# Expert tiles: a third weight buffer, and a ring of six chunks for the activations' parts

## The reference, cut to what matters

```
B, P, D, D_MLP, E, K = (2, 256, 128, 512, 8, 2)     # B is 16 in this run
gate_logits = jnp.einsum('bpd,de->bpe', x, W_gate)
top_w, top_idx = jax.lax.top_k(gate_logits, K)
...
for e in range(E):
    h = jax.nn.gelu(jnp.einsum('bpd,dm->bpm', x, W_in[e]) + b_in[e], approximate=False)
    y = jnp.einsum('bpm,md->bpd', h, W_out[e]) + b_out[e]
    out = out + combine[..., e, None] * y
```

## Time and profile before

| | |
|---|---|
| median of the runs | 4289.31 us |
| profiled execution | 4290.81 us |
| its span | 4289.0 us, mean granted clock of TensorE 0.963 |
| first two phases | to 3872 us |
| staging, gate, attention of the experts phase | 3872 to 4046 us |
| tile loop | 4046 to about 4256 us |
| last scatters, sums and the store | to 4289 us |
| PE busy over the span | 3967.9 us (93%) |
| DVE, ACT, POOL busy | 3516.5, 3105.0, 2004.2 us |

### The profile page before, as it was taken

How to read it: one execution, slowest core, us unless ns; L and a number is a source line. 1 busy time by engine, 2 the same in 40 slices (tenths; PEclk the granted TensorE clock), 3 DMA queues, 4 the chain that set the end, 5 groups by cost and what they waited for, 6 DMA issues and landing times. The chain is left out here.

```text
span 4289.0 us, 113558 instructions
## 1 busy us (share of the span) xinstructions
PE 3967.9 (93%) x42857; PEld 3167.1 (74%) x42857; DVE 3516.5 (82%) x6042; ACT 3105.0 (72%) x4915; POOL 2004.2 (47%) x1148
## 2 busy tenths in 40 slices
PE   6888689999999999999999999999999999988785
PEld 2444368888888888888888888788888888876664
DVE  7888688888888888888888888888888888864654
ACT  5888657777777777777777777777777777763453
POOL 0000165555555555555555555555555555523543
PEclk9999889999999999999999999999999999996887
DMA  2111142222333223322333232332323332324255
GB/s 86 45 36 37 40 132 66 68 69 64 86 71 74 66 64 89 75 65 67 73 85 72 64 69 68 85 71 68 72 65 80 78 70 64 71 51 154 82 166 173
DMA packets 365832, 330.60 MB, mean 77 GB/s; under 512 B 238096, under 2 KB 242576, under 8 KB 363600
## 3 DMA queue, kind: packets, MB, share of 16 engines
q1 hardware_dynamic: 360272, 312.74, 29.1%
q0 software_dynamic: 4992, 10.30, 0.7%
HBM read 69.33 MB, written 29.00 MB: 23 GB/s over the span
## 5 line engine op out<-in xcount | busy, mean ns | idle before, releaser
L705 POOL TENSOR_TENSOR qk_rotated<-qk_rotated,rotary_sines 128x1024 f32<-128x1024 f32 x384 | 924.1, 2406 | 1414.4 <-DVE rotary_sines L786 1414.4
L716 POOL TENSOR_TENSOR qk_rotated<-qk_rotated,rnorm 128x1024 f32<-128x1024 f32 x384 | 733.2, 1910 | 9.8 <-POOL qk_rotated L705 2.4
L794 DVE TENSOR_REDUCE qk_sumsq<-qk_squared 128x16 f32<-128x1024 f32 x384 | 465.0, 1211 | 97.6 <-ACT qk_squared L528 97.6
L235 PE MATMUL ps_proj<-qkv_w_hi,x_shifted_hi 128*128 128x512 f32 x1152 | 511.8, 444 | 15.8 <-DVE rotary_sines L786 11.3
L535 ACT ACTIVATE q_t<-ps_qk_t 128x512 f32<-128x512 f32 x384 | 229.5, 598 | 400.8 <-PE ps_qk_t L291 391.4
L776 DVE TENSOR_TENSOR qk_rotated<-ps_proj,rotary_scaled 128x1024 f32<-128x1024 f32 x384 | 467.0, 1216 | 7.9 <-ACT qk_squared L528 7.6
L786 DVE TENSOR_TENSOR rotary_sines<-ps_proj,rotary_scaled 128x1024 f32<-128x1024 f32 x384 | 465.9, 1213 | 1.7 <-POOL qk_rotated L705 1.7
L237 PE MATMUL ps_proj<-qkv_w_hi,x_shifted_lo 128*128 128x512 f32 x1152 | 459.6, 399 | 0.0
L549 ACT ACTIVATE k_t_by_head<-ps_qk_t 64x512 f32<-64x512 f32 x768 | 451.3, 588 | 11.0 <-PE ps_qk_t L300 1.6
L236 PE MATMUL ps_proj<-qkv_w_lo,x_shifted_hi 128*128 128x512 f32 x1152 | 455.9, 396 | 0.0
L316 PE MATMUL ps_scores<-k_t_by_head,q_t 128*32 128x128 f32 x12288 | 415.1, 276 | 10.1 <-ACT ps_scores L558 5.1
(11 more groups left out here) (309 smaller groups left out, 9083.8 us busy)
## 6 DMA issues: line engine op xcount, KB each, us to landing
v_by_window<-v_tokens SPq DMA_DIRECT2D x1152, 128.0 KB, 2.4
v_by_window<-v_tokens SPq DMA_DIRECT2D x384, 64.0 KB, 2.0
k_t_by_head<-k_t_by_head SPq DMA_DIRECT2D x96, 256.0 KB, 4.3
e_w_split<-expert_w_split SPq DMA_DIRECT2D x46, 512.0 KB, 4.7
v_by_window<-v_by_window SPq DMA_DIRECT2D x192, 64.0 KB, 2.0
qkv_w_raw<-in_layer_qk_dram SPq DMA_DIRECT2D x7, 1664.0 KB, 8.7
expert_rows<-in_slots_dram SPq DMA_DIRECT2D x1, 5980.0 KB, 24.7
e_tile_rows<-expert_rows SPq DMA_DIRECT2D x16, 260.0 KB, 4.5
```

The source lines that it names most:

```text
L235: mm(out, hi, HI[:, o:o + 512], start=True, stop=False)
L705: tt(u, u, TB[:], ALU.add).then_inc(added, 1)
L716: tt(u, u, r.unsqueeze(3).broadcast_to((P, 2, 8, DH)), ALU.mult).then_inc(scaled, 1)
L794: nc.vector.reduce_sum(SS[:, 16 * i:16 * i + 16], SQ[:].rearrange("p (h e) -> p h e", e=DH), AX).then_inc(sumsq, 1)
```

## The change

`WB` gets a third buffer, 8 KB of each partition. The room comes from `HHI` and `HLO`, each of which held the four chunks of two tiles (eight chunks) and now holds a ring of six chunks. The chunk of a tile is found by `ring(t, m)`. The semaphore `y_mm` now counts chunks and not tiles, so that ACT and DVE can wait for the chunk six back. A raw buffer goes too, as the staging has three places for an expert in place of four. SP's program loads the weights of tiles 0 and 1 ahead of the loop and in the loop those of tile t+2, where it loaded those of tile t. The loads of rows stay where they stood in the loop.

```diff
-NSTAGE = 4
+NSTAGE = 3
+NWB = 3
+NRING = 6
...
-        WB = [sb(f"w_split{k}", [P, 2, EHALF], F32R) for k in range(2)]
+        WB = [sb(f"w_split{k}", [P, 2, EHALF], F32R) for k in range(NWB)]
...
-        HHI, HLO = (sb(f"hidden_{x}", [P, 2, HM, BLK], F32R) for x in ("hi", "lo"))
-        WR = [sb(f"w_raw{k}", [P, EHALF])[:] for k in range(2)] + [H[:, k:k + 2, :].rearrange("p m x -> p (m x)") for k in (0, 2)]
+        HHI, HLO = (sb(f"hidden_{x}", [P, NRING, BLK], F32R) for x in ("hi", "lo"))
+        WR = [sb(f"w_raw{k}", [P, EHALF])[:] for k in range(2)] + [H[:, 0:2, :].rearrange("p m x -> p (m x)")]
...
+        def ring(t, m):
+            return (HM * t + m) % NRING
...
             def load_weights(t):
 
                 e = sp.value_load(EID[0:1, t:t + 1], min_val=0, max_val=E_ - 1)
-                if t >= 2:
-                    sp.wait_ge(h_out, HM * (t - 1))
-                sp.dma_start(EB[t % 4][:], expert_b[e]).then_inc(wi_in[t % 2], 16)
-                sp.dma_start(WB[t % 2][:, 0, :].bitcast(F32), split[e, :, 0:EHALF]).then_inc(wi_in[t % 2], 16)
-                if t >= 2:
-                    sp.wait_ge(y_out, t - 1)
-                sp.dma_start(WB[t % 2][:, 1, :].bitcast(F32), split[e, :, EHALF:2 * EHALF]).then_inc(wo_in[t % 2], 16)
-            load_weights(0)
+                if t >= NWB:
+                    sp.wait_ge(h_out, HM * (t - NWB + 1))
+                sp.dma_start(EB[t % 4][:], expert_b[e]).then_inc(wi_in[t % NWB], 16)
+                sp.dma_start(WB[t % NWB][:, 0, :].bitcast(F32), split[e, :, 0:EHALF]).then_inc(wi_in[t % NWB], 16)
+                if t >= NWB:
+                    sp.wait_ge(y_out, t - NWB + 1)
+                sp.dma_start(WB[t % NWB][:, 1, :].bitcast(F32), split[e, :, EHALF:2 * EHALF]).then_inc(wo_in[t % NWB], 16)
+            for t in range(NWB - 1):
+                load_weights(t)
             sp.wait_ge(scattered, 16 * NPOS)
             load_rows(0)
             for t in range(TILES):
                 if t + 1 < TILES:
                     load_rows(t + 1)
-                if t > 0:
-                    load_weights(t)
+                if t + NWB - 1 < TILES:
+                    load_weights(t + NWB - 1)
...
             def output(t, m):
-                b = t % 2
+                b, w, q = t % 2, WB[t % NWB], ring(t, m)
...
-                if m == HM - 1:
-                    last.then_inc(y_mm, 1)
+                mm(YB[b][:], w[:, 1, chunk(HM + m)], HHI[:, q, :], start=False, stop=(m == HM - 1)).then_inc(y_mm, 1)
...
             def hidden_high(t, m):
                 act.wait_ge(h_out, HM * t + m + 1)
-                after(act, y_mm, t - 1)
-                a(HHI[:, t % 2, m, :], H[:, m, :], ACT.Copy).then_inc(h_hi, 1)
+                after(act, y_mm, HM * t + m - NRING + 1)
+                a(HHI[:, ring(t, m), :], H[:, m, :], ACT.Copy).then_inc(h_hi, 1)
...
             def output(t):
-                dve.wait_ge(y_mm, t + 1)
+                dve.wait_ge(y_mm, HM * (t + 1))
```

More of the change, by code:

```diff
@@ L1719, in experts_phase @@
         shifted, bt_mm, base = sem("shifted"), sem("bt_mm"), sem("base")
-        xt_in, wi_in, wo_in = ([sem(f"{x}{k}") for k in range(2)] for x in ("xt_in", "wi_in", "wo_in"))
+        xt_in, (wi_in, wo_in) = [sem(f"xt_in{k}") for k in range(2)], ([sem(f"{x}{k}") for k in range(NWB)] for x in ("wi_in", "wo_in"))
         xp_mm, x_hi, x_lo, h_mm, h_out, h_hi, h_lo = (sem(x) for x in ("xp_mm", "x_hi", "x_lo", "h_mm", "h_out", "h_hi", "h_lo"))
@@ L1738, in staged @@
             k = e % NSTAGE
-            return h[:, k // 2, 2 * (k % 2):2 * (k % 2) + 2, :]
+            return h[:, 2 * k:2 * k + 2, :]
+        def ring(t, m):
+            return (HM * t + m) % NRING
         def halves(w):
@@ L1758, in _ @@
             for k in range(NSTAGE):
-                sp.wait_ge(w_saved[k], 32 * E_ // NSTAGE)
+                sp.wait_ge(w_saved[k], 32 * ((E_ - 1 - k) // NSTAGE + 1))
             sp.wait_ge(expert_ids, 1)
@@ L1953, in hidden @@
             def hidden(t, m):
-                b = t % 2
+                b, w = t % 2, WB[t % NWB]
                 if m == 0:
-                    pe.wait_ge(wi_in[b], 32 * (t // 2 + 1))
+                    pe.wait_ge(wi_in[t % NWB], 32 * (t // NWB + 1))
                     pe.wait_ge(x_hi, t + 1)
@@ L1960, in hidden @@
                     pe.wait_ge(hs_out, NBLK)
-                mm(HB[m][:], WB[b][:, 0, chunk(m)], XHI[b][:], start=True, stop=False)
-                mm(HB[m][:], WB[b][:, 0, chunk(HM + m)], XHI[b][:], start=False, stop=False)
+                mm(HB[m][:], w[:, 0, chunk(m)], XHI[b][:], start=True, stop=False)
+                mm(HB[m][:], w[:, 0, chunk(HM + m)], XHI[b][:], start=False, stop=False)
                 if m == 0:
                     pe.wait_ge(x_lo, t + 1)
-                mm(HB[m][:], WB[b][:, 0, chunk(m)], XLO[b][:], start=False, stop=True).then_inc(h_mm, 1)
+                mm(HB[m][:], w[:, 0, chunk(m)], XLO[b][:], start=False, stop=True).then_inc(h_mm, 1)
             def output(t, m):
-                b = t % 2
+                b, w, q = t % 2, WB[t % NWB], ring(t, m)
                 if m == 0:
-                    pe.wait_ge(wo_in[b], 16 * (t // 2 + 1))
+                    pe.wait_ge(wo_in[t % NWB], 16 * (t // NWB + 1))
                     after(pe, y_out, t - 1)
                 pe.wait_ge(h_lo, HM * t + m + 1)
-                mm(YB[b][:], WB[b][:, 1, chunk(m)], HHI[:, b, m, :], start=(m == 0), stop=False)
-                mm(YB[b][:], WB[b][:, 1, chunk(m)], HLO[:, b, m, :], start=False, stop=False)
-                last = mm(YB[b][:], WB[b][:, 1, chunk(HM + m)], HHI[:, b, m, :], start=False, stop=(m == HM - 1))
-                if m == HM - 1:
-                    last.then_inc(y_mm, 1)
+                mm(YB[b][:], w[:, 1, chunk(m)], HHI[:, q, :], start=(m == 0), stop=False)
+                mm(YB[b][:], w[:, 1, chunk(m)], HLO[:, q, :], start=False, stop=False)
+                mm(YB[b][:], w[:, 1, chunk(HM + m)], HHI[:, q, :], start=False, stop=(m == HM - 1)).then_inc(y_mm, 1)
             def rows_out(t):
@@ L2290, in hidden_low @@
                 dve.wait_ge(h_hi, HM * t + m + 1)
-                after(dve, y_mm, t - 1)
-                tt(HLO[:, t % 2, m, :], H[:, m, :], HHI[:, t % 2, m, :].bitcast(F32), ALU.subtract).then_inc(h_lo, 1)
+                after(dve, y_mm, HM * t + m - NRING + 1)
+                tt(HLO[:, ring(t, m), :], H[:, m, :], HHI[:, ring(t, m), :].bitcast(F32), ALU.subtract).then_inc(h_lo, 1)
             def output(t):
-                dve.wait_ge(y_mm, t + 1)
+                dve.wait_ge(y_mm, HM * (t + 1))
                 after(dve, yt_mm, t - 1)
```

## The result

The changed kernel takes 4377.85 us (median of 4 runs, 4375.58 to 4379.9) against 4289.27 us for the kernel before: 1.0209 times as long, interval [1.0191, 1.0227]. The forecast was 4373 us within 4325 to 4390.

The account below looks back on a forecast made before the run. The tile loop was taken as bound by PE, with holes waiting for weights. Late rows and slow clock make 13.5 us cycles: 82.5 us plus 0.8 for staging on 4290.8, less 1.5 to the median, gives 4373 us, range 4325 to 4390.

Parts of the forecast that it names:

- The rows are late next: SP's order in the tile loop: row loads now stand behind y_out of t-1, so rows land 5 us late in each tile.
- The cycle: Tile loop, rows_in to rows_in: 6.53 us to the out half, 0.43, 4.5, 0.04, plus 2.0 for the clock, 13.5 us.
- The clock: TensorE slows behind each row wait in the loop, adding 2.0 us to PE's part of each cycle, range 1.6 to 2.6.
- a rival of its own: TensorE's clock stays up despite the row waits in the loop: cycle 11.5 us, 4333 us; chance 0.12.
- The tail: Loop's end, rows_in(22) to the weighing of tile 20: 13.1 us, so that weighing comes 82.5 us later.
- the count: Late rows begin at tile 3: row load at 4060.8, rows_in(3) at 4065.3, then 19 cycles of 13.5 us to rows_in(22).
- Staging: Three staging places: expert 7's reload lands 0.2 to 1.4 us late for ACT; taken as 0.8 us, bounds 0 and 3.
- The rival of the rows in time: Rows land in time, the holes at L1961 go and nothing replaces them: 57 us less, 4232 us; chance 0.04.

Follow-up runs that it names:

- the kernel whose PE stays busy: The changed kernel with 16 more matmuls ahead of the wait for rows in each tile from the third; 4334.16 us, 1.0101 to the kernel before.
- rows_ahead: The changed kernel with load_rows(1) ahead of the loop and load_rows(t+2) in it, one tile further ahead; 4236.95 us, 0.9875 to the kernel before.
- `y_out` sooner: The changed kernel with DVE's bias add that counts y_out of t-1 moved ahead of the low part of chunk 2 of t; 4320.14 us, 1.0075.
- the row load first: The changed kernel with the row load issued between the wait for y_out and the out half; 4310.62 us, 1.0049 to the kernel before.

## Why the prediction was right

*The rows are late next.* Right in mechanism, place and size: 20 waits at `rows_in`, about 5 us each (98.0 us against "100 us in sum"), none for weights. Swapping two lines of the kernel before gives 4376.48 us; putting the rows ahead again takes the waits away.

*The cycle.* Predicted 13.5 us, measured 13.61. Its terms: rows_in to the out half 8.5 against 8.72 us, of which 6.53 at the full clock; 0.43 to the row load (0.44); 4.5 to land (4.47 with PE's start). The sum of the terms at full clock, 11.5, is shown by itself by the kernel whose PE stays busy, 11.55.

*The clock.* Predicted 2.0 us a cycle from two weight waits of before, measured 2.06 by that same kernel. This was the term with the widest bounds and a rival of its own (4333 us, which is where that kernel lies, 4334).

*The tail.* From rows_in(22) to the weighing of tile 20, 13.1 predicted, 13.2 measured (4326.48 to 4339.69). That weighing came 87.3 us later than in the earlier trace rows, and so did the end of the span (4376.3 against 4289.0), against 82.5 predicted. Of the 4.8 us between them 2.6 are the start of the phase, which lay that much later in the profiled execution (3874.92 against 3872.30 us, before anything that was changed), and 19 x 0.11 = 2.1 the cycle. The start of the phase lies between 3869.5 and 3874.9 us over all ten profiles here, whatever the kernel, so the 2.6 us is no error of the prediction. One number of the count doesn't follow as written: 4061.80 less the hole of 1.15 us is 4060.65 and not 4060.8. It makes 0.15 us.

*Staging.* Wrong by its 0.8 us: it costs nothing. I took the landing of the loads of before for the reload of expert 7, at the late end of what the chain could hide; measured, ACT takes up expert 7 at the same time.

*The rival of the rows in time.* 4232 us was worked out for a kernel whose rows are in time; `rows_ahead` is that kernel, and took 4236.95. The rival was wrong for this change only in the point that the prediction named: what stands ahead of the row load on SP.

## What to carry to other kernels

A load queue that waits in its own program makes every load inherit the waits of all that stand ahead of it. When one stream is moved further ahead, write down for each other stream which wait now stands right before it, and how far that is from its use. A wait for DMA on TensorE is paid twice when the engine is on the chain, once as idle time and once as slow clock behind it; with `y_out` sooner the waits went from 4.9 to 3.0 us and the cycle from 13.61 to 10.56, so 3.05 us came back for 1.9 us of idle time, since the clock was low for less of the time.

## What the runs showed of the hardware that I had not expected

After the 19 waits of 4.7 to 5.1 us in the changed kernel's loop the transposes that came next were at the slow clock each time (1.11 or 1.12 us long as shown). After the 20 waits with the row load first, all but one of 2.6 to 3.2 us, they were so in 13 cycles (0.98 us and more). With `y_out` sooner, after 18 waits of 2.8 to 3.2 us and two longer ones, they were so in 9, and in three more the clock fell during them or behind them (from 4098.02, 4121.25 and 4132.39). The length of the wait alone doesn't tell which: the whole cycle behind a wait of 3.63 us (from 4236.85) ran at the full clock there, and with the row load first the transposes behind a wait of 2.57 us (4243.47) were slow.

PE's own part of a cycle, which is the cycle less the wait at its end, shows the price. It is 6.6 to 6.7 us where the clock stayed up, in 6 of the 19 cycles with the row load first and in 8 of the 19 with `y_out` sooner. In the others of both it is 7.9 to 8.2 us (once 9.4), and in the changed kernel 8.6 to 8.8 in all but the first. In the mean it is 7.5, 7.5 and 8.7 us, so the clock costs some 0.9, 0.9 and 2.1 us a cycle at waits of 2.7, 3.0 and 4.9 us: the price falls faster than the wait.

A 260 KB load lands in 2.8 us with no weight half right ahead of it and in 4.5 us with 512 KB asked for 0.44 us ahead of it on the same queue (medians). Asking for the smaller, more urgent one first cost the larger one nothing that showed: the out halves land in 3.9 us in the median there, and in 4.3 us in the changed kernel.
